# Two low-part tiles by an adding DMA, a thirteenth split tile, and one activation series for the first layer in a recommender kernel

## What is computed

```
def _cin_layer(h, h0, W, b):
    Wr = W.reshape(W.shape[0], Hn, Mn)
    x = jnp.einsum('bhd,bmd,ohm->bod', h, h0, Wr) + b[None, :, None]
    return jax.nn.relu(x)
...
h0 = e                                   # (1024, 32, 64)
x1 = _cin_layer(h0, h0, W1, b1)          # 128 rows out of 32*32 products
next_hidden = x1[:, :64]
direct1 = x1[:, 64:]
direct2 = _cin_layer(next_hidden, h0, W2, b2)   # 128 rows out of 64*32 products
z = jnp.sum(jnp.concatenate([direct1, direct2], axis=1), axis=-1)
h = jnp.concatenate([z, dense_ctx], axis=1)
h = jnp.maximum(h @ W_top1 + b_top1, 0.0)
h = jnp.maximum(h @ W_top2 + b_top2, 0.0)
y = h @ W_top3
```

## Time and profile before

| | us |
|---|---|
| median of 3 runs (lowest, highest) | 2048.58 (2048.46, 2048.8) |
| the profiled execution | 2048.25 |
| its span, first to last instruction | 2046.3 |
| PE busy | 2016.5 (99%) |
| DVE busy | 1979.8 (97%) |
| ACT busy | 1635.1 (80%) |
| POOL busy | 1524.9 (75%) |

### The profile page before, as it was taken

One profiled execution on the slowest core, in us unless ns is written; L12 is line 12 of the kernel. 1 busy time (PEld: TensorE's weight loads), 2 busy tenths in 40 slices (PEclk: granted clock), 3 DMA queues, 4 the chain that ended last, 5 costly groups with the idle time before them and its releaser, 6 DMA issues.

```text
span 2046.3 us, 28743 instructions
## 1 busy us (share of the span) xinstructions
PE 2016.5 (99%) x6910; PEld 1299.9 (64%) x6910; DVE 1979.8 (97%) x543; ACT 1635.1 (80%) x4758; POOL 1524.9 (75%) x580
## 2 busy tenths in 40 slices
PE   5999999999999999999999999999999999999999
PEld 2666666666666666666666666666666666666664
DVE  6999999999999999999999999999999999999992
ACT  4688888888888888888888888888888888888883
POOL 4778778778778778778778778778778778778520
PEclk9999999999999999999999999999999999999999
DMA  7677777767777777777777777776777777777740
GB/s 237 183 218 202 210 205 201 211 204 196 215 205 200 210 206 200 210 207 195 215 207 199 208 209 199 212 206 193 217 207 198 209 209 198 210 208 199 209 118 0
DMA packets 239330, 406.50 MB, mean 199 GB/s; under 512 B 33377, under 2 KB 50273, under 8 KB 239090
## 3 DMA queue, kind: packets, MB, share of 16 engines
q1 hardware_dynamic: 231026, 397.10, 67.0%
q0 software_dynamic: 8192, 8.40, 2.0%
HBM read 321.49 MB, written 16.78 MB: 165 GB/s over the span
## 4 chain that ended last, share of the span: by engine, by line
DVE 60%; issue 35%; PE 3%; DVEq 0%; DMA 0%; ACT 0%; POOL 0%; SPq 0%; ACTq 0%; POOLq 0%
DVE pnear L472 27%; DVE pfar L472 16%; DVE plo L477 16%; PE acc L544 0%; PE x1p L633 0%; PE acc L567 0%; PE acc L633 0%; PE acc L540 0%; PE acc L556 0%; PE acc L557 0%; DMA x1rep<-x 0%; POOL gathered L242 0%; PE x1p L515 0%; PE acc L640 0%; ACT phi L726 0%
## 5 line engine op out<-in xcount | busy, mean ns | idle before, releaser
L242 POOL DMA_INDIRECT gathered<-in_tables,idx x256 | 766.2, 2993 | 104.8 <-issue 53.0
L263 POOL TENSOR_TENSOR prod<-near,h 128x2048 f32<-128x2048 f32 x126 | 577.3, 4582 | 177.0 <-PE acc L547 175.0
L726 ACT CAST phi<-pnear 128x4096 fp32r<-128x4096 f32 x128 | 465.8, 3639 | 265.6 <-DVE pnear L472 265.6
L556 PE MATMUL acc<-phi,w2lo 128*128 128x512 f32 x1536 | 601.5, 392 | 1.3 <-ACT phi L726 1.3
L557 PE MATMUL acc<-phi,w2hi 128*128 128x512 f32 x1536 | 601.1, 391 | 0.0
L659 ACT ACTIVATE acc<-acc,bias 128x64 f32<-128x64 f32 (+1 forms) x2048 | 576.3, 284 | 8.1 <-PE acc L557 4.9
L472 DVE TENSOR_TENSOR pfar<-far,x1p 128x4096 f32<-128x4096 f32 x128 | 565.9, 4421 | 11.5 <-PE acc L567 3.6
L477 DVE TENSOR_TENSOR plo<-pnear,phi 128x4096 fp32r<-128x4096 f32 x128 | 568.7, 4443 | 0.0
L472 DVE TENSOR_TENSOR pnear<-near,x1p 128x4096 f32<-128x4096 f32 x128 | 564.7, 4412 | 3.5 <-ACT x1p L703 3.5
L544 PE MATMUL acc<-prod,w1T 128*128 128x512 f32 x1024 | 462.7, 595 | 6.0 <-issue 4.5
L567 PE MATMUL acc<-pfar,w2T 128*128 128x512 f32 x1024 | 460.3, 592 | 0.0
(11 more groups left out here) (70 smaller groups left out, 542.5 us busy)
## 6 DMA issues: line engine op xcount, KB each, us to landing
near<-emb_rows SPq DMA_DIRECT2D x512, 256.0 KB
far<-emb_rows SPq DMA_DIRECT2D x512, 256.0 KB, 4.1
x1rep<-x SPq DMA_DIRECT2D x256, 256.0 KB, 4.3
h<-emb_rows SPq DMA_DIRECT2D x128, 256.0 KB
emb_rows<-gathered SPq DMA_DIRECT2D x128, 128.0 KB, 3.5
gathered<-in_tables,idx POOLq DMA_INDIRECT x256, 5.0
rem_a<-emb_rows SPq DMA_DIRECT2D x64, 64.0 KB
rem_b<-emb_rows SPq DMA_DIRECT2D x64, 64.0 KB
```

The source lines that it names most:

```text
L242: nc.gpsimd.indirect_dma_start(out=gathered[s][:, g, :], out_offset=None, in_=a["tables"], in_offset=bass.IndirectOffsetOnAxis(ap=idx[s][: ...
L263: nc.gpsimd.tensor_tensor(prod1[:, :, :], near[(u + 2) % 3][:, :, :], h0[odd][:, :].unsqueeze(1).to_broadcast([P, K1, N]), ALU.mult).then_ ...
L556: nc.tensor.matmul(acc2[s][:, :], w2lo[:, t, :], phi[:, t, :], start=(t == 0), stop=False)
L726: nc.scalar.copy(phi[:, 0:T_NEAR, :], pnear[:, :, :, :].rearrange("p a k n -> p (a k) n")).then_inc(hi_near_ready, 1)
```

## The change

Four things are changed together.

- **Low parts by DMA.** For the near tiles 0 and 1 ACT writes -tile, rounded to fp32r, into `plo` (an activation Copy with scale -1.0), and POOL issues a DMA that adds the fp32 tile to it (`low_parts`, 128 x 1024, 512 KB read beside the bytes that it adds to). The sum is the low part. DVE's subtraction for the near tiles covers six tiles in place of eight. ACT makes `phi` near in two pieces (tiles 2 to 7, then 0 and 1), and PE takes them in that order.
- **13 tiles split.** The first tile of the second four far tiles is split as well: the far `phi` and `plo` cover five tiles, `whole` three.
- **One series for layer 1.** `hidden1` and `direct1` become `layer1(c, s)` on ACT: eight activations over 128 rows which write `x1` (now 128 rows) and the sums at once, at the start of the step. The semaphore `x1_ready` goes; SP waits for `z1_ready`. The sums go to `sums1`, and DVE copies them into `z1` in two halves, in steps 126 and 127. `top1(0)` moves from step 126 to step 127.
- **Remainder rows in the even step.** SP loads them at the end of the even step, not near the start of the odd one, and the store of gathered rows comes before the far rows.

```
+T_DMA = 2
+T_FAR = T_NEAR + K2
+T_SPLIT = T_FAR + 1
+T_WHOLE = T_NEAR + A2 * K2 - T_SPLIT
...
+            def low_parts(c):
+                pool.wait_ge(minus_ready, c + 1)
+                pool.sem_inc(lo_begun, 1)
+                nc.gpsimd.dma_start(plo[:, 0:T_DMA, :], pnear[:, 0, 0:T_DMA, :], accum_op=ALU.add
+                                    ).then_inc(lo_dma_in, 16)
...
@@ POOL, step: behind the multiplication that makes prod1
+                low_parts(c)
                 if odd and within(at, 3):
                     remainder_products(pair + 2)
...
@@ DVE, step
                 if begun(at):
                     dve.wait_ge(lo_near_ready, c)
+                    dve.wait_ge(lo_dma_in, 16 * c)
                 products2(pnear[:, :, :, :], near[u % 3][:, :, :], odd, K1).then_inc(pnear_ready, 1)
...
-                low(slice(0, T_NEAR), pnear[:, :, :, :]).then_inc(lo_near_ready, 1)
+                low(slice(T_DMA, T_NEAR), pnear[:, :, :, :].rearrange("p a k n -> p (a k) n")[:, T_DMA:T_NEAR, :]).then_inc(lo_near_ready, 1)
...
@@ PE, step
-                high(odd, range(0, T_NEAR)).then_inc(hi_near_used, 1)
+                high(odd, range(T_DMA, T_NEAR))
+                pe.wait_ge(hi_dma_ready, c + 1)
+                high(odd, range(0, T_DMA)).then_inc(hi_near_used, 1)
...
                     pe.wait_ge(z1_ready, CHUNKS - 1)
-                    top1(0)
                 else:
                     pe.wait_ge(z1_ready, CHUNKS)
+                    pe.wait_ge(sums1_copied, 1)
+                    top1(0)
                     top1(1)
...
                 whole(odd).then_inc(far_used, 1)
+                pe.wait_ge(lo_dma_in, 16 * c + 16)
+                low(odd, range(0, T_DMA)).then_inc(lo_dma_used, 1)
                 pe.wait_ge(lo_near_ready, c + 1)
-                low(odd, range(0, T_NEAR))
+                low(odd, range(T_DMA, T_NEAR))
...
@@ ACT
-            def relu_sums(acc, bias, rows, z, c, ready):
+            def relu_sums(out, acc, bias, z, c, ready):
                 for b in range(CB):
                     cols = slice(b * D, (b + 1) * D)
-                    ins = nc.scalar.activation(acc[rows, cols], acc[rows, cols], ACT.Relu, bias=bias[rows, :],
-                                               accum_out=z[rows, bass.ds(c * CB + b, 1)])
+                    ins = nc.scalar.activation(out[:, cols], acc[:, cols], ACT.Relu, bias=bias[:, :],
+                                               accum_out=z[:, bass.ds(c * CB + b, 1)])
                 ins.then_inc(ready, 1)
...
-                nc.scalar.copy(phi[:, 0:T_NEAR, :], pnear[:, :, :, :].rearrange("p a k n -> p (a k) n")).then_inc(hi_near_ready, 1)
+                products = pnear[:, :, :, :].rearrange("p a k n -> p (a k) n")
+                if begun(at):
+                    act.wait_ge(lo_dma_used, c)
+                nc.scalar.activation(plo[:, 0:T_DMA, :], products[:, 0:T_DMA, :], ACT.Copy, scale=-1.0).then_inc(minus_ready, 1)
+                nc.scalar.copy(phi[:, T_DMA:T_NEAR, :], products[:, T_DMA:T_NEAR, :]).then_inc(hi_near_ready, 1)
+                nc.scalar.copy(phi[:, 0:T_DMA, :], products[:, 0:T_DMA, :]).then_inc(hi_dma_ready, 1)
```

More of the change, by code:

```diff
@@ L363, in step @@
                     replicate_x1()
[L364 to L368, removed]
                 if within(at, 3):
@@ L373, in step @@
                     load_near((c + 3) * N, 1 - odd, u % 3)
+                if not odd and within(at, 5):
+                    store_rows(pair + 2, (u // 2 + 2) % 3, turn + (u // 2 + 2) // 3 + 1)
                 if within(at, 2):
@@ L440, in _, with low_weights @@
                 nc.vector.tensor_copy(z1[0:DENSE, h * N:(h + 1) * N], tp[h][0:DENSE, :]).then_inc(tp_copied, 1)
[L442 to L446, removed]
+            def low_weights(n):
+                tiles = PARTS[n]
+                hi, lo = (flat(w[:, tiles.start:tiles.stop, :]) for w in (w2hi, w2lo))
+                dve.wait_ge(part_hi, n + 1)
+                nc.vector.tensor_tensor(lo, tp[n % 2][:, 0:len(tiles) * O], hi.bitcast(fp32), ALU.subtract).then_inc(tp_copied, 1)
             def products1(s, ks):
@@ L466, in _ @@
             products1(1, slice(0, K1)).then_inc(p1_ready, 1)
-            for h in range(1, T_SPLIT // K1):
-                low_weights(h)
+            for n in range(2, len(PARTS)):
+                low_weights(n)
             def products2(out, h0part, s, k):
@@ L476, in low @@
             def low(parts, whole):
-                return nc.vector.tensor_tensor(plo[:, parts, :], whole.rearrange("p a k n -> p (a k) n"),
-                                               phi[:, parts, :].bitcast(fp32), ALU.subtract)
+                return nc.vector.tensor_tensor(plo[:, parts, :], whole, phi[:, parts, :].bitcast(fp32), ALU.subtract)
             def step(c, turn, u, at):
@@ L555, in high @@
                 for t in parts:
-                    nc.tensor.matmul(acc2[s][:, :], w2lo[:, t, :], phi[:, t, :], start=(t == 0), stop=False)
+                    nc.tensor.matmul(acc2[s][:, :], w2lo[:, t, :], phi[:, t, :], start=(t == T_DMA), stop=False)
                     mm = nc.tensor.matmul(acc2[s][:, :], w2hi[:, t, :], phi[:, t, :], start=False, stop=(t == T_SPLIT - 1))
@@ L565, in whole @@
             def whole(s):
-                for k in range(K2):
-                    mm = nc.tensor.matmul(acc2[s][:, :], w2T[:, k, :], pfar[:, 1, k, :], start=False, stop=False)
+                for k in range(T_WHOLE):
+                    mm = nc.tensor.matmul(acc2[s][:, :], w2T[:, k, :], pfar[:, 1, K2 - T_WHOLE + k, :], start=False, stop=False)
                 return mm
@@ L687, in _, with high_weights @@
             last.then_inc(near_staged, 1)
-            def high_weights(h):
-                act.wait_ge(tp_filled, 6 + h)
-                nc.scalar.copy(flat(w2hi[:, K1 * h:K1 * (h + 1), :]), tp[1 - h % 2][:, :]).then_inc(part_hi, 1)
+            def high_weights(n):
+                tiles = PARTS[n]
+                act.wait_ge(tp_filled, 5 + n)
+                nc.scalar.copy(flat(w2hi[:, tiles.start:tiles.stop, :]), tp[n % 2][:, 0:len(tiles) * O]).then_inc(part_hi, 1)
             high_weights(0)
+            high_weights(1)
             remainder_hi(0)
@@ L696, in _ @@
             act.wait_ge(acc1_ready, 1)
-            hidden1(0)
-            for h in range(1, T_SPLIT // K1):
-                high_weights(h)
-            direct1(0, 0)
+            layer1(0, 0)
+            for n in range(2, len(PARTS)):
+                high_weights(n)
             def copy_x1rep(s):
@@ L719, in step @@
                     act.wait_ge(x1rep_in, 16 * A2 * c + 16 * A2)
-                    hidden1(1 - odd)
+                    layer1(c + 1, 1 - odd)
                 if not odd and at != 0 and within(at, 2):
@@ L736, in step @@
                     act.wait_ge(acc2_ready, c)
-                nc.scalar.copy(phi[:, T_NEAR:T_SPLIT, :], pfar[:, 0, :, :]).then_inc(hi_far_ready, 1)
+                nc.scalar.copy(phi[:, T_NEAR:T_SPLIT, :], pfar[:, :, :, :].rearrange("p a k n -> p (a k) n")[:, 0:T_SPLIT - T_NEAR, :]).then_inc(hi_far_ready, 1)
                 if at == 0:
```

53 lines of the change are left out of this document (33 added, 20 removed).

## The result

The changed kernel takes 2072.46 us, median of 5 runs (2067.7 to 2079.52), against 2048.8 us before (2048.46 to 2049.12): a ratio of 1.012 (1.010 to 1.014). It is **1.2% slower**; forecast was 2031, 0.86% faster. The profiled execution has a span of 2077.7 us (before 2046.3) and a mean granted clock of 0.992 (before 0.998). It is the slowest of the five (2079.52 us), 7 us over the median; the other four have 0.993 to 0.996.

A forecast was written before the change was run, and what follows sets the result against it. PE was taken as the bound, its period falling from 15.36 to 15.19 us; 2046.3 + 2.0 (start) + 1.7 (end) - 21.0 (126 periods) made a 2029.0 us span, 2031 us with the 1.95 beside it; range 2024 to 2075 us.

The forecast's parts named there:

- PE without gaps: Sign that the forecast is right: PE stays full in the steady part, with `pnear` starts 15.19 us apart.
- the ring: ACT and DVE, from the end of `pnear` through `phi` and `plo` far to the next: 15.06 us, 0.13 under the period.
- Rival 3: Ring of ACT and DVE 0.15 to 0.3 us longer than summed: no change, 2052 us; 13% together with rival 2.
- rival 1: The adding DMA lands late and DVE waits before `pnear`: slower, 2094 us if landing takes 10.2 us; chance 15%.
- the 0.67 us between pieces: Adding DMA's landing: four 256 KB pieces 0.67 us apart behind a first of 4.1, with 1.0 for issue: 7.1 us.
- the 9.4 us: Time from the adding DMA's issue until DVE's next `pnear` wants to start, waiting for the landing; 2 us left.
- 79 to 89: DMA engines: forecast load in percent, up from 67%, the higher if the bytes added to are counted too.
- The replication of x1: SP's DMAs of `x1`, ready 1.8 us later, were to land before ACT wants them, 0.4 us left at the median.
- rival 2: `x1` is replicated late and ACT waits before `x1p`: no change, 2051 us at 5.5 us landing; 13% together with rival 3.
- nothing gained: SP's new order of remainder, store and near loads was to bring no gain and no loss.
- The end: End of the run: `top1(0)`, 1.72 us, moves from step 126 onto the path in step 127: +1.7 us.
- This part hides, with 0.2 us left in the even step.: ACT's layer-1 series, remainder casts, -tile and six tiles of `phi` end at 15.0 us against PE's need at 15.19.

The follow-up runs named there:

- the small DMA: The changed kernel with its adding DMA moving 16 columns of one tile in place of 1024 columns, 8 KB in place of 512 KB: 2055.16 us, ratio 1.0035.

## Why the prediction was wrong

The sum went by one period times 126. The difference between the spans of the two executions with a trace, 2077.7 - 2046.3 = 31.4 us, against -17.3 in the forecast, splits by the first and the last `pnear` (36.40 and 1993.42 before, 38.88 and 2020.64 after) into start, middle and end:

| part | forecast | measured |
|---|---|---|
| start | +2.0 | +2.5 |
| 127 intervals | -21.0 | +24.7 |
| end | +1.7 | +4.2 |

- **PE: right for the period.** 15.36 to 15.19 us: between the turns `pnear` comes 15.14 to 15.22 us apart (median of all intervals 15.22). "PE without gaps" wasn't so: it has 20.
- **DVE and the ring: right.** Idle before `plo` far 0.42 us, 46.3 us over the run. That the ring holds 15.19 with 0.13 us to spare was true in the changed kernel. Its terms were not all safe: `plo` near takes 3.35 us (3.27 from start to start, as forecast) or 3.82, the longer where it meets POOL's operation. Rival 3 named the sign that was then seen, PE waiting for `phi` and nobody for a DMA, but its ring isn't the cause: ordinary periods keep to 15.19.
- **The adding DMA: right.** Its issue took 0.99 us (forecast 1.0), and DVE waited once, 0.9 us, for its landing: rival 1 did not come. The time to landing itself has no row, nor has the 0.67 us between pieces in the sum; what is shown is that it fits into the 9.4 us in all steps but one. The DMA engines are at 84.7% by the two big queues, inside the 79 to 89 forecast. Queue 0 had 8.40 MB and 2.0% before; with the adding DMA it has 75.52 MB and 21.7%, so 19.7/67.12 = 0.29% a MB, against 63.0/397.10 = 0.159% in queue 1: 1.8 times as much. The Trainium skill (Collectives: The Full Stack, The bandwidth ceiling) says that an add reads two sources; the 1.8 fits that, here for a DMA from SBUF to SBUF, but no run tells it from other differences between the two queues.
- **The replication of x1: right.** 13 waits and 9.6 us in the whole run; rival 2 did not come.
- **POOL, SP: right for this change**, but "nothing gained" was too little: the new order of SP's steps saves 20 us against the old one beside the same DMA.
- **The end: 2.5 us short.** PE's wait for `phi` in step 127 is 3.46 us, 2.4 more than the 1.06 before, and the sum had only `top1(0)`.
- **ACT: this is the step that failed.** "This part hides, with 0.2 us left in the even step." It was summed over one ordinary pair of steps. But 18 times in a run ACT goes from the end of its loop's body to its beginning, and the first instruction there comes 1.9 us late on average. Less the 0.2 us that makes 1.7 x 18 = 31 us; PE's waits there add up to 30.2, and the lower clock after seven of them to 11. No rival had it: the forecast for slow cases rested on the adding DMA and the replication. That the range held the time (2072.46 in 2024 to 2075) is luck: it reached so far for the price of other mechanisms.

It could have been seen. The table of waits of the kernel before has "ACT x L664 <- issue: 11.8, 8, 1.6", a wait that no ordinary step of that kernel shows, ahead of the very operation that was moved onto the tight path. Six steps in place of two give the 1.06 to 1.61 us, and with them alone the sum would have been 18 x (0.87 - 0.2) = 12 us worse, 2043 us (0.87 is the mean of these over the ordinary 0.47). The rest, that `x` is 1.9 us late and not 0.9 in the changed kernel, no row of before shows. The traffic of the adding DMA is 0.7 us of it (1.2 with the small one); the last 0.3 us isn't explained.

With ACT's turns made rare the time comes near the forecast, 12.1 of the 17.6 us of gain: 2036.44 us against 2031, and a span of 2034.0 against 2029.0. Of these 5 us 3.7 are in the intervals (two turns among them) and 1.4 at the end.

## What to carry to other kernels

Read the longest period of the program, not the shortest: a loop of six steps has its own hiccup in each round, and slack of 0.2 us in one step is none if a turn takes 2. When an engine's cover is spent, look up its waits marked "issue", find at which steps they stand and where they are longer than in the other steps, and price them without the cover. A longer loop body on that one engine is then the cheap remedy (18 turns to 2, 36 us here), and bytes added to the DMA queues are paid also by engines that issue none of them.

## What the hardware showed

- The turn of ACT's loop: 1.06 to 1.61 us before the next instruction in the kernel before, 2.98 to 3.18 us with 512 KB of adding DMA in each step and the same ACT code, 2.67 to 3.76 us in the changed kernel, 1.35 to 2.27 us in that kernel without the one series, with the same adding DMA. Counted from PE's result, or from ACT's last instruction where that came later, the means are 1.0 us before, 3.1, 2.1 and 1.8, and 1.4 with the small DMA; an ordinary step has 0.1 to 0.2 where it waits for PE. So the traffic alone doesn't set the length. Entering the loop and leaving it cost nothing like it (0.57 us before `x` in step 6, 1.34 in step 120 of the changed kernel). That it is the fetch of code is the reading that fits (queue q14 carries 0.87 MB in 106 packets, and 0.52 MB in 64 where ACT's loop turns twice); no run shows the fetch itself.
- TensorE's granted clock fell to 0.59 in the 4 us stretch that begins 1.7 us after a gap of 1.96 us, and was 1.00 again in the next. Read in the same way behind each of PE's gaps (from 1.5 to 5 us after its end), it is 1.00 after the gaps of 0.94 to 1.74 us, 0.51 to 0.72 after those of 2.20, 2.03 (twice), 1.96 (twice), 1.95 and 1.93 us, 0.50 after the 3.46 us of step 127, and 1.00 after two of 2.00 and 2.01 us. The matmuls of the low stretch were 0.43 us apart in place of 0.23.
- A multiplication on POOL of 32 x 512 took 1.30 us while DVE made `pfar` (one operand in PSUM), and 3.60 us beside DVE's subtraction (1009.35 us, kernel with SP's old order). The subtraction that was already running kept its 3.35 us; the next one, which began before POOL was done, took 3.48 in place of 2.83 us.
